# Softmax denominators turned by TensorE before and after one small reciprocal

## The reference

```python
scores = jnp.einsum('bhqd,bhkd->bhqk', q, k) / jnp.sqrt(jnp.float32(HEAD_DIM))
scores = scores + causal
attn = jax.nn.softmax(scores, axis=-1)
out = jnp.einsum('bhqk,bhkd->bhqd', attn, v)
out = out.transpose(0, 2, 1, 3).reshape(B, S, D_MODEL)
return out @ wo + bo
```

## Time and profile before

| | |
|---|---|
| median of 3 runs | 512.5 us (510.59 to 512.6) |
| profiled execution, own time | 513.89 us |
| its span, first to last instruction | 512.2 us |
| mean granted TensorE clock, as a share of full | 0.95 |
| busy: TensorE, VectorE, GpSimd, ScalarE | 452.9, 338.7, 185.7, 162.8 us |
| instructions | 10468 |

### The profile page before, as it was taken

One profiled execution on the slowest core, in us unless ns is written; L12 is line 12 of the kernel. 1 busy time (PEld: TensorE's weight loads), 2 busy tenths in 40 slices (PEclk: granted clock), 3 DMA queues, 4 the chain that ended last, 5 costly groups with the idle time before them and its releaser, 6 DMA issues.

```text
span 512.2 us, 10468 instructions
## 1 busy us (share of the span) xinstructions
PE 452.9 (88%) x3270; PEld 421.5 (82%) x3270; DVE 338.7 (66%) x898; ACT 162.8 (32%) x394; POOL 185.7 (36%) x447
## 2 busy tenths in 40 slices
PE   0618698999999999999999999999999999998651
PEld 0507698999999999989898989899999999998531
DVE  8595534467767777776868686776768685745541
ACT  3303133234333333333333333332424242424100
POOL 7250312232434333334352524334352526161332
PEclk9997689799999999999999999999999999999956
DMA  3152726281827274636455554636283727410000
GB/s 116 43 101 81 125 83 134 73 146 62 143 70 145 67 144 71 148 63 155 64 148 77 126 99 115 110 107 118 95 130 95 118 81 142 73 33 1 10 1 21
DMA packets 130980, 47.83 MB, mean 93 GB/s; under 512 B 103165, under 2 KB 127233, under 8 KB 130954
## 3 DMA queue, kind: packets, MB, share of 16 engines
q1 hardware_dynamic: 127882, 43.31, 39.8%
q10 hardware_dynamic: 2304, 2.10, 2.9%
q0 software_dynamic: 768, 2.10, 1.3%
HBM read 30.71 MB, written 14.68 MB: 89 GB/s over the span
## 4 chain that ended last, share of the span: by engine, by line
PE 81%; DVE 6%; SPq 4%; DMA 3%; issue 2%; ACT 2%; POOL 1%; ACTq 0%; POOLq 0%; DVEq 0%
PE ps_pv L833 29%; PE ps_a L810 12%; PE ps_b L800 10%; PE ps_m L746 6%; PE ps_m L747 5%; PE ps_m L748 5%; PE ps_m L766 3%; PE ps_a L785 2%; PE ps_b L785 2%; SPq L317 2%; PE ps_n L841 2%; DVE ident_bf L544 1%; PE ps_n L881 1%; DVE w_in L506 1%; DMA q_plain<-max_rows 1%
## 5 line engine op out<-in xcount | busy, mean ns | idle before, releaser
L833 PE MATMUL ps_pv<-probs,v_diag 128*128 128x256 f32 (+7 forms) x1024 | 186.1, 317 | 2.1 <-ACT probs L452 1.6
L833 PEld LDWEIGHTS ps_pv<-probs,v_diag 128*128 128x128 f32 x1024 | 148.2, 194 | 8.4 <-ACT probs L452 3.5
L452 ACT ACTIVATE probs<-ps_b 128x512 f32<-128x512 f32 (+4 forms) x176 | 90.0, 520 | 161.5 <-PE ps_b L785 161.2
L608 DVE TENSOR_REDUCE row_max<-ps_a 128x2 f32<-128x512 f32 (+2 forms) x192 | 101.6, 548 | 36.0 <-PE ps_a L785 35.7
L810 PE MATMUL ps_a<-k_plain,q_diag 128*128 128x96 f32 (+7 forms) x512 | 98.3, 304 | 5.0 <-DVE row_max L608 4.4
L800 PE MATMUL ps_b<-q_plain,k_diag 128*128 128x96 f32 (+7 forms) x512 | 99.0, 300 | 2.7 <-DMA k_diag<-plain_parts 1.7
L403 POOL COPY v_diag<-v_rows 32x64 f32<-32x64 f32 x256 | 60.1, 235 | 73.3 <-PE ps_pv L833 43.5
L810 PEld LDWEIGHTS ps_a<-k_plain,q_diag 128*128 128x128 f32 x512 | 76.8, 205 | 7.4 <-DVE row_max L608 4.9
L800 PEld LDWEIGHTS ps_b<-q_plain,k_diag 128*128 128x128 f32 x512 | 75.8, 195 | 4.4 <-DMA k_diag<-plain_parts 1.8
L376 POOL TENSOR_TENSOR rot_lo<-rot,rot_hi 128x512 fp32r<-128x512 f32 x16 | 20.3, 1269 | 130.4 <-ACT rot_hi L471 103.1
L593 DVE TENSOR_REDUCE y_sel<-ps_m 128x128 f32<-128x1024 f32 x32 | 39.2, 1225 | 35.6 <-PE ps_m L766 35.1
(11 more groups left out here) (135 smaller groups left out, 690.9 us busy)
## 6 DMA issues: line engine op xcount, KB each, us to landing
plain_parts<-rot_hi SPq DMA_DIRECT2D x64, 128.0 KB, 2.1
k_plain<-plain_parts SPq DMA_DIRECT2D x16, 384.0 KB
q_diag<-plain_parts SPq DMA_DIRECT2D x64, 96.0 KB
q_plain<-plain_parts SPq DMA_DIRECT2D x16, 384.0 KB
k_diag<-plain_parts SPq DMA_DIRECT2D x64, 96.0 KB
plain_parts<-rot_lo SPq DMA_DIRECT2D x32, 128.0 KB, 2.1
x_in<-in_L_attn_x_dram SPq DMA_DIRECT2D x16, 128.0 KB, 3.8
q_plain<-max_rows ACTq DMA_DIRECT2D x16, 128.0 KB, 4.2
```

Of the source, the lines that this page charges most:

```text
L452: act.activation(probs[:, k % PR, 0:cols], ps_b[k % 2][:, 0:cols], ACT.Exp, scale=SCALE)\
L608: last = dve.tensor_reduce(row_max[:, NBLK - 1 - j, groups[0]:groups[-1] + 1], scores[:, :, col:col + width(j)], AX.X, ALU.max)
L833: mm = pe.matmul(ps_pv[:, g // 2, BLK * j:S], v_diag[q][:, j, 128 * g:128 * g + 128], probs[:, k % PR, col:col + width(j)], start=(j == 0 ...
```

## The change

The sums are no longer inverted in their 128 x 256 layout, in which each value stands eight times. TensorE multiplies each half of `sums`, as the stationary operand, by a new constant `one_row` with a one for the first row of each head. Out comes the transposed tile with 16 columns, one a head, for each half: 128 x 32 in `ps_n`, columns 320 to 351. VectorE inverts these 32 columns from PSUM in one instruction. ScalarE widens them, each head's value copied to eight columns (`inv_wide`, 128 x 256). TensorE turns the two halves back by multiplying with the identity, into `ps_n` columns 256 to 511, and the multiplication into `attn` reads that. All four matmuls are plain fp32.

In the programs: TensorE has the first turn at the end of slot 1, before its slots 2 and 3, waiting for `sums_copied`, and the turn back in slot 2 behind that slot's scores, waiting for `widths_done`. ScalarE has the widening in slot 1, behind the weighted copies and in front of the first exponential, waiting for `den_done`. VectorE has one reciprocal in slot 1, waiting for `sumst_ready`. The constants' table grows by 16 columns.

```diff
                     ("stacked", BLK), ("head_cols", 128), ("head_is", GH), ("tie", E), ("one_row", H), ("max_sel", H)):
...
-        inv_den = sb("inv_den", [128, S])
+        inv_den, inv_wide = sb("inv_den", [128, 2, H]), sb("inv_wide", [128, 2, 128])
...
+        ps_sumst = ps_n[:, 320:320 + 2 * H].rearrange("p (t h) -> p t h", t=2)
+        ps_inv = ps_n[:, 256:256 + S]
...
+                    if slot == 1 and has(d):
+                        after(act, "den_done", d, 1, 1)
+                        act.activation(inv_wide[:, :, :].rearrange("p t (h i) -> p t h i", i=HD),
+                                       inv_den[:, :, :].unsqueeze(3).broadcast_to([128, 2, H, HD]), ACT.Copy)\
+                            .then_inc(s_["widths_done"], 1)
...
-                    if slot in (1, 2) and has(d):
-                        after(dve, "sums_copied", d, 1, 1)
-                        half_cols = slice(128 * (slot - 1), 128 * slot)
-                        dve.reciprocal(inv_den[:, half_cols], sums[:, half_cols]).then_inc(s_["den_done"], 1)
+                    if slot == 1 and has(d):
+                        after(dve, "sumst_ready", d, 1, 1)
+                        dve.reciprocal(inv_den[:, :, :], ps_sumst).then_inc(s_["den_done"], 1)
                     if slot == 2 and has(d):
 
                         after(dve, "pv_copied", d, 1, 1)
                         after(dve, "y_ready", d)
-                        after(dve, "den_done", d, 2, 2)
-                        dve.tensor_tensor(attn[:, :], weighted[:, :], inv_den[:, :], ALU.mult).then_inc(s_["normed"], 1)
+                        after(dve, "invt_ready", d, 1, 1)
+                        dve.tensor_tensor(attn[:, :], weighted[:, :], ps_inv, ALU.mult).then_inc(s_["normed"], 1)
...
+                    if slot == 1 and has(d):
+                        after(pe, "sums_copied", d, 1, 1)
+                        for t in range(2):
+                            mm = pe.matmul(ps_sumst[:, t], sums[:, 128 * t:128 * t + 128], C("one_row"), start=(t == 0),
+                                           stop=True, skip_group_check=True)
+                        mm.then_inc(s_["sumst_ready"], 1)
+                    if slot == 2 and has(d):
+                        after(pe, "widths_done", d, 1, 1)
+                        for t in range(2):
+                            mm = pe.matmul(ps_inv[:, 128 * t:128 * t + 128], inv_wide[:, t, :], C("ident"), start=(t == 0),
+                                           stop=True, skip_group_check=True)
+                        mm.then_inc(s_["invt_ready"], 1)
...
+    put("one_row", p[:, None] == HD * np.arange(H)[None, :])
```

More of the change, by code:

```diff
@@ L57, in _layout @@
     for name, w in (("ident", 128), ("before", 128), ("cos", S), ("sin", S), ("mask_a", BLK), ("mask_b", BLK),
-                    ("stacked", BLK), ("head_cols", 128), ("head_is", GH), ("tie", E), ("max_sel", H)):
+                    ("stacked", BLK), ("head_cols", 128), ("head_is", GH), ("tie", E), ("one_row", H), ("max_sel", H)):
         CONSTS[name] = (at, w)
@@ L196, in layer_kernel @@
         names += """b_ready exp_done pv_ready""".split()
-        names += """pv_copied sums_copied den_done normed xb_done y_ready z1_done st1_done mv1_done ve1_done
+        names += """pv_copied sums_copied sumst_ready den_done widths_done invt_ready normed xb_done y_ready z1_done st1_done mv1_done ve1_done
                     rs1_done x1_done""".split()
```

## The result

The changed kernel takes 525.09 us (median of 4 runs, 524.23 to 527.35) against 511.54 us of the kernel before (4 runs, 509.49 to 512.6): ratio 1.0277, interval 1.0226 to 1.0327. It is slower by 13.6 us. The forecast was 20.8 us more, 533; the measured median lies 0.09 us inside the lower edge of the range given, 525 to 542, and outside the range that the likeliest case had for itself, 529 to 542.

The account below looks back on a forecast made before the run. TensorE's queue was taken to fill the 26.63 us step. Steps 3 to 15 add 18.1 us, step 2 0.9, step 16 1.1 and step 17 0.7, together 20.8, giving 533 us, range 525 to 542.

Parts of the forecast that it names:

- the likeliest case: Whole kernel: TensorE's new passes and waits lengthen the steps; 533 us, own range 529 to 542, chance 0.75.
- the rival in which only the work counts: All sequences: new waits are covered, only added TensorE work costs, 0.88 us a sequence, 526.5 us; chance 0.14.
- The old waits at the boundary: Between two steps, slot 1's scores to slot 3's product: TensorE already waits 0.46 us in the kernel before.
- Prices of the pieces: Added per sequence: eight passes of 0.11 us, one reciprocal of 348 ns, one widening of 0.38 us.
- The chain of waits: Step boundary: TensorE waits 0.24 us for sums, then 0.37 for widths; the old wait for the exponential is swallowed.
- If a pair is waited for, its first weight load is exposed: 1.13 - 0.95 = 0.18: Both turns on TensorE: a waited-for pair of calls takes 0.18 us more before its passes.
- the 1.39: Steps 3 to 15: slot 3's product ends at 255.37 instead of 253.98, so each step is 1.39 us longer.
- so the turn back costs its 0.44 at half clock: 0.9: Step 2: first turn fits into a 1.66 us load wait, the turn back costs 0.9 us at low clock.
- 1.1: Step 16, without A scores: product ends at 464.51 instead of 463.44, 1.1 us more.
- VectorE sets the step: All steps: 1.52 us less VectorE comes off each of 13 steps, 20 us in all, 493 us; chance 0.02.
- No change: Step boundary: new work falls wholly into waits, needing 0.88 us of waiting where 0.46 is; chance 0.03.
- The clock falls at each boundary: Every step boundary: TensorE's clock drops to half, 3 us each, 39 us in all, above 560 us; chance 0.04.

Follow-up runs that it names:

- dve_relief2: Kernel before with each reciprocal cut to 16 of its 128 columns, nothing else changed: step 26.60 us against 26.63, ratio 0.997.
- work_only2: Kernel before with the four added matmuls in their places, fed from constants, waiting for nothing and read by nobody: step 27.10 us, ratio 1.0147.
- before2: Kernel before, unchanged, profiled a second time: step 26.63 us, mark of step 2 at 94.91 us, ratio 1.0027.
- wait_only2: Kernel before with only TensorE's wait for the sums copy added at the end of slot 1, no matmul: step 26.79 us, ratio 1.001.
- fill2: Kernel before with the value projection and transposes of x moved from slot 6 to slot 3, ahead of the product: step 26.75 us, ratio 1.003.
- one_pass2: Changed kernel with the four matmuls' operands in fp32r, one pass each instead of two: step 27.52 us, ratio 1.0157 to the kernel before.
- spread2: Changed kernel with all its pieces one slot later: step 27.27 us, ratio 1.012 to the kernel before.
- bridge: Kernel before with 16 passes of idle matmuls at the end of slot 1 of step 2 alone: median 508.14 us, ratio 0.995.
- bridge_tail: As bridge, with further idle matmuls ahead of four TensorE waits in the last step: median 504.84 us, ratio 0.9877 to the kernel before.
- after2: Changed kernel, unchanged, profiled a second time: step 27.84 us, mark of step 2 at 90.72 us, ratio 1.0318 to the kernel before.

## Why the prediction was right, and where its sizes were off

The mechanism was right in the middle of the kernel, and the traces show it piece by piece. That the number fell within the range was luck in part. The lower edge, 525, came from the rival in which only the work counts, and that rival fell. The median of 525.09 is nearer to that rival's price, 526.5, than to the forecast's 533. What brought it down there is a lead of about 4 us at the start that no term had; without it the time would have been an estimated 529 (525.09 + 4.2).

**What bounds the kernel.** Right. dve_relief2 took 0.03 us off the step for 1.4 us less of VectorE; work_only2 lengthened it by 0.47 for 0.89 us more of TensorE.

**The old waits at the boundary.** Right: 0.46 was read, 0.45 stood on the load queue, and work_only2 used up 0.42 of them.

**Prices of the pieces.** The reciprocal was 357 ns with PSUM as its source (348 forecast). dve_relief2 has one of 16 columns from SBUF at 240 ns; between that and 936 for 128, one of 32 columns from SBUF is an estimated 339, which leaves about 18 ns for PSUM. The multiplication takes 421 ns with one operand in PSUM, 424 with both in SBUF. The Trainium skill, VectorE: DVE Perf Modes, section on the TRN2 errata, gives 120 fixed cycles for a PSUM source against 58 for SBUF, an estimated 60 ns more; this trace shows less. The widening was 417 ns (380). A pass held the queue for 0.11, at 16 columns too (0.45 for four), 0.89 for all eight. The Trainium skill, TensorE: Matmul & The Clock Gate, section Back-to-back issue gap, has about 81 ns for a weight load and matmul of 128 columns in a stream, which gives an estimated 0.65 for eight; these plain fp32 passes took longer. The 0.085 that the prediction read for line 881 comes from the chain; on the load queue its loads, too, start 0.11 apart.

**The chain of waits.** Right in place and order: TensorE stops for the sums, then for the widths, and the old wait for the exponential goes. 0.24 and 0.37 were forecast. Measured on the load queue the two waits are 0.41 and 0.39; the profile, which counts from the end of the pass before, puts 0.20 and 0.19 beside the matmuls.

**The term that was mis-sized in the middle** is "If a pair is waited for, its first weight load is exposed: 1.13 - 0.95 = 0.18". It was added twice, once to each turn, and stands once in the end before, 252.85 + 1.13 = 253.98, from which the 1.39 was counted. But 1.13 and 0.95 are both distances in a chain in which a group is counted from the end of the one before it, and the 0.95 owes its shortness to that overlap. From load to load the product takes 0.75 after a wait (252.85 to 253.60) and 0.77 without one (253.48 to 254.25 in the changed kernel), and a pair behind a wait held the queue for 0.45 and 0.44. Without the 0.18 the first turn's result is ready at 251.43 + 0.62 = 252.05 instead of 252.23, and everything behind it is 0.18 earlier; the widths are there at 252.93, the turn back is off the queue at 253.37 and slot 3's A at 254.05. There the product's load starts, where it started at 252.85 before: the same chain, from load to load, gives 1.20 a step. Over 13 steps the difference from 1.39 is 2.5 us of the overshoot.

**The term that was wrong at the start** is step 2: "so the turn back costs its 0.44 at half clock: 0.9". It took the low clock of the earlier trace rows as given. It was the consequence of the wait of 1.66 us in the same row. In every profile of a kernel in which that wait stands (before, before2, work_only2, wait_only2, dve_relief2, fill2; 1.35 to 2.2 us) the clock is low in the next stretch; where it is gone or short (changed kernel twice, one_pass2, spread2 with 0.26, bridge, bridge_tail with 0.22) it isn't. The clock is worth 3.1 us, by bridge against before2. In after2 the first B scores also start 1.94 earlier, and the changed kernel's own turns take part of both back, so the lead is 4.2. The 0.9 us that the forecast added turned into a gain of 4.

**The end.** 1.39 + 1.1 + 0.7 = 3.2 was forecast from mark 14 to mark 17; 0.84 + 2.51 + 0.86 = 4.2 was measured (1.18 + 2.52 + 0.81 in the second pair). The term that was too small is that of step 16, "1.1", since the clock fell in that step of the changed kernel. Its stretch from 470 to 480 us in the first profile (PE, PEld, DVE, ACT and POOL busy, granted clock, DMA share, GB/s):

```profile
470.00:480.00 10.00, 9.48 (x54) 8.40 (x53) 3.09 (x11) 4.08 (x9) 0.95 (x2) 0.83 0.01 2
```

Both profiles show it, behind waits of 0.86 and 0.52 us for the sums and the widths. But one_pass2 has the same two waits there (0.86 and 0.51) and kept 1.00, and so did the kernel before behind its single wait of 1.57. Mark 15 to mark 16 takes 26.47 and 26.49 us in the changed kernel and 24.46 in one_pass2. What decides it is open. The forecast had priced a falling clock only as a rival for all steps.

**The sum.** For before2 and after2: -4.2 to the mark of step 2, +14.5 over twelve steps, +4.5 from mark 14 to mark 17 and -0.3 behind it come to the difference of their spans, 525.0 - 510.5 = 14.5 us. The forecast had +0.9 and 16.7 for the first two, 3.2 for the third.

**The rivals.** "Only the work counts" fell: work_only2 has 0.47 of the 1.20, and spread2, with the same work and no waits for it, 0.64. "VectorE sets the step" fell with dve_relief2. "No change" fell: the ratio's interval begins at 1.0226. "The clock falls at each boundary" fell: it was 1.00 from 120 to 450 us in both profiles of the changed kernel.

**What stays open.** Why TensorE doesn't wait for `k_diag` in step 2 of the changed kernel. It reaches the B scores 0.85 us later than the kernel before would, which alone doesn't cover a wait of 1.4 to 2.1, and work_only2, 0.45 later, still waited for 1.35. The load's issues ran from 79.45 to 82.83 in after2 and from 80.70 to 85.19 in before2, and what made them quicker was not tested.

## What to carry to other kernels

Work taken off an engine that has time to spare is worth nothing; what it costs elsewhere is paid in full: here 1.5 us less of VectorE a step were bought with 0.9 us of TensorE and two waits. When a value has to go round over several engines, put each hop a slot later than it could be at the earliest: the same hops cost 1.21 us a step where TensorE had to wait for its two turns, and 0.64 where it did not. Even so the change loses here. To price a wait, measure from weight load to weight load, and look what the clock does after it: a gap of 1.35 to 2.2 us was followed by 3.4 to 6.8 us at half the clock in one place, and not in another.

## What the runs showed of the hardware that was not expected

- TensorE idled for 1.35 to 2.2 us in step 2 and then had a granted clock of 0.50 for 6.8 us in five profiles and for 3.4 in fill2 (in before2 0.4 + 4.0 + 2.5, from 0.95, 0.50 and 0.69 in the three stretches of 4 us). With the gap filled by matmuls that nobody reads, the same work ran at 1.00 and took 3.84 us instead of 6.92. At the end of the kernel the same remedy gave 3.3 us in the median.
- A gap of that length doesn't always do it: in step 16 TensorE idled for 1.57 us in before, before2, dve_relief2, fill2, bridge and bridge_tail, and the clock stayed at 1.00 each time. What sets the two places apart is open.
- Waits of 0.41 and 0.39 us in every step, 1.5 us apart, never lowered the clock between 120 and 450 us.
- A plain fp32 matmul's pass with 16 columns holds TensorE's queue for as long as one with 128 (0.45 and 0.44 us for four), though its record is shorter (268 and 319 ns).
- In wait_only2, whose added wait has no matmul of its own behind it, TensorE went on 0.22 to 0.37 us after the release (0.22 twice, 0.33 and 0.37 at four boundaries); in the changed kernel, with a matmul behind the same wait, 0.04 us after.
